# Project stage of a state-space and transformer kernel: matmuls to delta, B, C two tiles behind, statistics behind the taps, a wait in the load queue

## What is computed

```python
x = x + jnp.tanh(g_xattn[0]) * _L0_xattn_ref(ctx_1024, _layernorm(x, axis=-1), ...)
# inside, per batch b
x = jnp.einsum('ed,bld->bel', in_proj_w, hidden_states)      # 1024 channels from 512
xc = depthwise causal convolution of x, 4 taps
u = jax.nn.silu(xc + conv_b[None, :, None])
x_dbl = jnp.einsum('ke,bel->bkl', x_proj_w, u)               # 64 rows: delta's 32, B's 16, C's 16
delta = jax.nn.softplus(jnp.einsum('er,brl->bel', dt_proj_w, dt_lo) + dt_proj_b[None, :, None])
...                                                          # scan over l, then
y = y * jax.nn.silu(z)                                       # z is the layer norm of x
```

## Time and profile before

| what | us |
|---|---|
| median of 3 runs | 3019.37 (3013.48 to 3019.66) |
| time of the profiled execution | 3018.8 |
| its span | 3017.1 |
| project stage in it | about 172 |

### The profile page before, as it was taken

One profiled execution on the slowest core, in us unless ns is written; L12 is line 12 of the kernel. 1 busy time (PEld: TensorE's weight loads), 2 busy tenths in 40 slices (PEclk: granted clock), 3 DMA queues, 4 the chain that ended last, 5 costly groups with the idle time before them and its releaser, 6 DMA issues. The chain is left out here.

```text
span 3017.1 us, 30047 instructions
## 1 busy us (share of the span) xinstructions
PE 2392.6 (79%) x10552; PEld 1599.2 (53%) x10552; DVE 2110.9 (70%) x2626; ACT 1338.0 (44%) x2470; POOL 1683.2 (56%) x600
## 2 busy tenths in 40 slices
PE   7857777778777547986888888888883299999998
PEld 3334444444444326653767666654552186668863
DVE  4569999999999674432999999999997633310000
ACT  3457755566655342242665555665552212410000
POOL 1169999999999401003998898999993100000000
PEclk9969999989999758998999999999997599999999
DMA  7722252342522396745236335336333543144543
GB/s 259 253 90 75 67 158 77 113 139 63 164 66 60 115 374 208 287 134 189 84 105 197 99 104 186 109 98 216 98 108 133 204 170 98 50 144 151 152 153 104
DMA packets 224869, 426.70 MB, mean 141 GB/s; under 512 B 17488, under 2 KB 101712, under 8 KB 221904
## 3 DMA queue, kind: packets, MB, share of 16 engines
q1 hardware_dynamic: 211216, 368.68, 38.3%
q10 hardware_dynamic: 12160, 51.39, 4.3%
q0 software_dynamic: 1344, 4.72, 0.4%
HBM read 340.84 MB, written 83.89 MB: 141 GB/s over the span
## 5 line engine op out<-in xcount | busy, mean ns | idle before, releaser
L600 POOL TENSOR_TENSOR s_x<-s_du,k_bB 128x2048 f32<-128x2048 f32 x256 | 1156.3, 4533 | 80.8 <-PE s_py L663 52.0
L896 ACT ACTIVATE s_pA<-s_delta,k_negA 128x512 f32<-128x512 f32 x1024 | 664.1, 680 | 382.7 <-DVE s_x L947 373.9
L663 PE MATMUL s_py<-k_ident,s_x 128*128 128x128 f32 x4096 | 582.8, 289 | 260.6 <-DVE s_x L947 253.2
L663 PEld LDWEIGHTS s_py<-k_ident,s_x 128*128 128x128 f32 x4096 | 506.8, 150 | 489.3 <-DVE s_x L947 347.2
L962 DVE TENSOR_TENSOR_SCAN s_pA<-s_pA,s_x 128x512 f32<-128x512 f32 x384 | 452.2, 1214 | 40.9 <-POOL s_x L600 38.3
L947 DVE TENSOR_TENSOR s_x<-s_pA,k_bC 128x1024 f32<-128x1024 f32 x384 | 464.2, 1209 | 19.1 <-DMA k_bC<-scratch_xd 19.0
L962 DVE TENSOR_TENSOR_SCAN s_pA<-s_pA,s_carry,s_x 128x512 f32<-128x512 f32 x384 | 472.6, 1275 | 2.0 <-POOL s_x L600 1.6
L1570 PE MATMUL l_p<-l_hT,l_ring 128*128 128x256 f32 x1792 | 397.0, 381 | 2.5 <-DVE l_hT L1784 1.4
L1570 PEld LDWEIGHTS l_p<-l_hT,l_ring 128*128 128x128 f32 x1792 | 341.9, 191 | 50.2 <-issue 2.0
L607 POOL TENSOR_TENSOR s_x<-s_hp,k_bC 128x1024 f32<-128x1024 f32 x128 | 302.2, 2361 | 15.8 <-DVE s_hp L962 15.5
L1577 PE MATMUL l_p<-l_ring,l_hidden 128*128 128x512 f32 x512 | 220.9, 592 | 1.7 <-DMA l_ring<-in_wo 1.7
(11 more groups left out here) (200 smaller groups left out, 3100.1 us busy)
## 6 DMA issues: line engine op xcount, KB each, us to landing
k_bB<-scratch_xd SPq DMA_DIRECT2D x32, 1024.0 KB, 11.8
k_bC<-scratch_xd SPq DMA_DIRECT2D x32, 1024.0 KB, 12.3
scratch_ug<-p_ug ACTq DMA_DIRECT2D x16, 1024.0 KB, 4.0
k_u<-scratch_ug SPq DMA_DIRECT2D x64, 256.0 KB, 3.6
s_gy<-scratch_ug SPq DMA_DIRECT2D x64, 256.0 KB, 4.2
s_xt<-in_x SPq DMA_DIRECT2D x64, 256.0 KB, 4.6
scratch_x<-s_xt SPq DMA_DIRECT2D x64, 256.0 KB, 3.2
r_x<-scratch_x SPq DMA_DIRECT2D x32, 512.0 KB, 11.4
```

Source lines behind the costliest of these rows:

```text
L600: pool.tensor_tensor(out=x[:, 4 * g:4 * g + 4], in0=du[:, s % 2:s % 2 + 1].broadcast_to([P, 4, HALF]), in1=bB[:, 4 * g:4 * g + 4], op=ALU. ...
L663: last = nc.tensor.matmul(py[:, a], x[:, n, a * P:(a + 1) * P], ident[:], is_transpose=True, start=False, stop=is_last and a == HALF // P - 1)
L896: nc.scalar.activation(pA[:, n % 4], delta[:, s % 2], ACT.Exp, scale=negA[:, s % NE, n:n + 1]).then_inc(dA_ready, 1)
```

## The change

- `x_dbl(k - 2)` instead of `x_dbl(k - 1)` stands behind the projection of tile k, with a buffer more for u and the gate: `U_BUFS` is 3. `X_AHEAD` goes from 8 to 6.
- The three taps of a tile stand in a row, and all statistics of the next tile behind the third.
- SyncE waits for the second half of the first context before it loads more than `conv`. The x tile 0 now goes ahead of the rest of `w_in`. `w_x` has a semaphore of its own, for which TensorE alone waits, ahead of X(0).
- `copy_out(0)` stands behind tile 9's work instead of tile 8's.

```diff
-X_AHEAD = 8
+X_AHEAD, U_BUFS = 6, 3
...
-    ug = sb("ug", [P, 2, 2, L])
+    ug = sb("ug", [P, U_BUFS, 2, L])
...
+            sp.dma_start(conv[:], t["conv"]).then_inc(weights, 16)
+            sp.wait_ge(ctx_first[1], 16)
+            load_x(0)
             sp.dma_start(w_in[:, :, 2 * P:], t["w_in"][:, :, 2 * P:]).then_inc(w_in_rest, 16)
-            load_x(0)
+            sp.dma_start(w_x[:], t["w_x"]).then_inc(w_x_in, 16)
             load_x(1)
-            sp.dma_start(conv[:], t["conv"]).then_inc(weights, 16)
-            sp.dma_start(w_x[:], t["w_x"]).then_inc(weights, 16)
...
-                if k == 0:
-                    pe.wait_ge(weights, 32)
-                else:
-                    x_dbl(k - 1)
-            x_dbl(STEPS_NOW - 1)
+                if k == 2:
+                    pe.wait_ge(w_x_in, 16)
+                if k >= 2:
+                    x_dbl(k - 2)
+            for k in range(STEPS_NOW - 2, STEPS_NOW):
+                x_dbl(k)
...
-            act.wait_ge(weights, 32)
+            act.wait_ge(weights, 16)
...
-                at_least(act, ug_out[j], 16 * (k // 2))
-                at_least(act, xd_sums, k - 1)
+                at_least(act, ug_out[n], 16 * (k // U_BUFS))
+                at_least(act, xd_sums, k - U_BUFS + 1)
...
-                if k == NE:
+                if k == NE + 1:
                     copy_out(0)
...
-                    if i == 0 and k == 0:
-                        make_shift(0)
-                    if k + 1 < STEPS_NOW:
-                        (take_stats, take_mean, make_shift)[i](k + 1)
+                if k + 1 < STEPS_NOW:
+                    take_stats(k + 1)
+                    take_mean(k + 1)
+                    make_shift(k + 1)
```

More of the change, by code:

```diff
@@ L125, in project_stage @@
     ps_d = ctx.enter_context(nc.psum_tensor("p_xdp", [H2 * ND, HALF], F32))
-    w_in_ready, w_in_rest, weights, ctx_in = sem("w_in_r"), sem("w_in_rest"), sem("weights"), sem("ctx1")
+    w_in_ready, w_in_rest, weights, w_x_in, ctx_in = sem("w_in_r"), sem("w_in_rest"), sem("weights"), sem("w_x_in"), sem("ctx1")
     ctx_first = [sem(f"ctx0{h}") for h in range(H2)]
@@ L132, in project_stage @@
     u_ready, gate_ready, xd_sums, xd_copied, xd_out = sem("u"), sem("gate"), sem("xd_sums"), sem("xd_copied"), sem("xd_out")
-    ug_out = [sem(f"ug_out{j}") for j in range(2)]
+    ug_out = [sem(f"ug_out{j}") for j in range(U_BUFS)]
     exponent, small, made, kept, kept_chain = (sem(n) for n in ("exponent", "small", "made", "kept", "kept_chain"))
@@ L168, in _ @@
             sp.wait_ge(xd_out, 32 * SPAN)
-            for j in range(2):
-                sp.wait_ge(ug_out[j], 16 * STEPS_NOW // 2)
+            for j in range(U_BUFS):
+                sp.wait_ge(ug_out[j], 16 * len(range(j, STEPS_NOW, U_BUFS)))
         @block.gpsimd
@@ L193, in x_dbl @@
                 for h in range(H2):
-                    last = nc.tensor.matmul(ps_d[h * ND:(h + 1) * ND, :], w_x[:, e, :], halves(ug[:, k % 2, 0], h),
+                    last = nc.tensor.matmul(ps_d[h * ND:(h + 1) * ND, :], w_x[:, e, :], halves(ug[:, k % U_BUFS, 0], h),
                                             start=e == 0, stop=e == NE - 1)
@@ L229, in copy_out @@
                                   xd[h * ND:(h + 1) * ND]).then_inc(xd_out, 16)
-            act.wait_ge(weights, 32)
+            act.wait_ge(weights, 16)
             act.wait_ge(pads, 2)
             for k in range(STEPS_NOW):
-                e, j = k % NE, k % 2
+                e, j, n = k % NE, k % 2, k % U_BUFS
                 act.wait_ge(projected, k + 1)
@@ L283, in _ @@
                     take_mean(0)
-                    dve.wait_ge(weights, 32)
+                    make_shift(0)
+                    dve.wait_ge(weights, 16)
                     dve.wait_ge(pads, 2)
@@ L290, in _ @@
                         dve.wait_ge(taps, 3 * k + i)
-                    nc.vector.scalar_tensor_tensor(out=ug[:, j, 0], in0=raw[:, j, i:i + L], scalar=conv[:, e, i:i + 1],
-                                                   in1=ug[:, j, 0], op0=ALU.mult, op1=ALU.add).then_inc(taps, 1)
-                    if i == 0 and k == 0:
-                        make_shift(0)
-                    if k + 1 < STEPS_NOW:
-                        (take_stats, take_mean, make_shift)[i](k + 1)
+                    nc.vector.scalar_tensor_tensor(out=ug[:, n, 0], in0=raw[:, j, i:i + L], scalar=conv[:, e, i:i + 1],
+                                                   in1=ug[:, n, 0], op0=ALU.mult, op1=ALU.add).then_inc(taps, 1)
+                if k + 1 < STEPS_NOW:
+                    take_stats(k + 1)
+                    take_mean(k + 1)
+                    make_shift(k + 1)
 NPAIR = NS // 2
```

8 lines of the change are left out of this document (4 added, 4 removed).

## The result

| | before | changed |
|---|---|---|
| median of 5 runs, us | 3015.84 (3013.48 to 3019.66) | 2995.95 (2987.73 to 2998.47) |
| ratio, 95% interval | | 0.9924 (0.9904 to 0.9943) |
| profiled execution, us | 3018.8 | 2988.98 |
| its span | 3017.1 | 2987.3 |
| next stage starts at | 172.33 | 151.78 |

The kernel is faster by 19.9 us by the medians and by 22.9 us by the ratio. The forecast was 3000.1, a gain of 19.3. Two questions are open at this point: whether the steps inside the stage were right, and where the other 9.2 of the 29.8 us between the two profiled spans come from, since the next stage starts only 20.55 us earlier.

A forecast was written before the change was run, and what follows sets the result against it. The prediction took ScalarE and VectorE, passing one tile back and forth, to bound the project stage. Statistics 17.4, silu(0) 1.3 and an earlier start 0.6 sum to 19.3 us: from 3019.4 to 3000.1, range 2994 to 3007.

The forecast's parts named there:

- The ring of ScalarE and VectorE: Project stage: the two engines pass one tile back and forth and set the pace, 9.00 us a tile.
- The statistics: Moved behind VectorE's taps: 1.24 us less in each of 14 tiles, 17.4 us, plus 1.3 us at silu(0).
- cover: VectorE's 3.80 us wait before its first tap, said to hide the estimated 2.6 us of statistics at no cost.
- The lead of TensorE: Projections finish 2.8 us before ScalarE needs them, shrinking 0.29 us a tile, 0.5 left at tile 10, lasting to the end.
- The third buffer: One more buffer for u: ScalarE's first tap waits for a store three tiles old, not two; effect nothing.
- The head: Stage start, new load order: TensorE starts at 9.3 instead of 10.10; 0.6 us gained, from -0.6 to 2.3.
- off the path: At P(1): removing TensorE's 0.71 us wait for `w_x` was said not to affect the stage's time.
- the slow phase of P(0): TensorE's first five records or so, at half speed; starting 0.8 us earlier was to give 0.4 to 0.8 us.
- The sum: 17.4 + 1.3 + 0.6 = 19.3 us gained, giving 3000.1 from the median of 3019.4.
- the spread of the runs: Range term for whole executions: up to 6 us below the median.
- the rivals: TensorE as bound 0.16 (3005); late loads at the start 0.10 (3006.8); gain lost behind the stage 0.03 (3019); slow clock 0.03 (3116).

The follow-up runs named there:

- the head alone: Kernel before with only SyncE's wait, x tile 0 ahead of the rest of `w_in` and `w_x`'s own semaphore, run twice: 3023.03 and 3016.45 us.
- the third's: Changed kernel, unchanged, third profile and third set of times: ratio to the kernel before 0.992 (0.9907 to 0.9934), median 2990.95 us.

## Why the prediction was right, and where it failed

**What bounds.** Right. The ring of ScalarE and VectorE set the pace: the statistics alone brought 14.3 us, the matmuls two behind alone nothing.

**The statistics.** Right in size: 7.76 us a tile forecast and measured, silu(0) 1.3 us nearer to its first tap. Their cover is 1.37 us wide, where 3.80 - 2.6 gave 1.2, and the experiment with more statistics went through it.

**The lead of TensorE.** Right. The forecast took 8.05 us for TensorE's tile, and measured are 8.07; it had 0.5 us left at tile 10, and measured are 0.9, of which 0.3 come from the pause of ScalarE behind silu(7). That pause stood in no term of the forecast and cost 0.3 us. Behind the copy the lead lasted as said, down to 0.14 us at tile 15. TensorE's wait there was 1.62 us, not 1.3, and its clock did not fall.

**The third buffer.** "Nothing" was right for the changed kernel, but the reason given, that no store had held ScalarE before, says nothing of a faster ring. Statistics alone, with two buffers, lost 1.68 us to a store.

**The head.** 0.8 us earlier was taken for TensorE's start and 0.6 of it for the stage. Over all profiles the start is 0.5 us earlier, and silu(0), set right for the statistics, 0.3: 26.2 on average in the seven profiles with wait and late statistics, against 26.5 in the four with the old queue (three of them less 1.32). The first profile of the changed kernel had 2.1. The sentence that the removed wait for `w_x` is "off the path" was wrong for the head alone: it makes a gap behind which the clock falls, for 1.9 us, and in the changed kernel P(2) fills the gap. That 2.58 MB had moved when a load with 1.57 MB up to its end landed is what the trace shows; that the later loads took its time was not tested, and whether wait or order brings the half microsecond stays open. For the slow phase of P(0) the forecast had that a start 0.8 us earlier gives 0.4 to 0.8; measured, the phase lasts 3 to 6 us by itself, which moves silu(0) by more than the shift of the start does.

**The sum.** The stage gained 20.55 us in the first pair of profiles and 19.2 us by the means of two and three, against 19.3 forecast. That the mean comes so near is in part luck, since the start of the next stage moves by 0.9 us in the kernel before and by 1.6 in the changed one. The three ratios say 22.9, 17.8 and 24.1 us; the forecast's gain is inside their intervals but for the third's, 0.9907 to 0.9934, which begins at 19.9 us.

**What failed** is the step from the gain to a time, and with it the range. The sum's 19.3 us were taken from a level of 3019.4, the median of three runs ("That execution lies 0.6 below the median of 3019.4"). That level was high: the five runs of the first set have their median at 3015.84, and the later sets of the kernel before have 3015.33, 3015.53 and 3013.73, so it is 4 to 6 us lower. The same 19.3 us from 3015 give 2996, and the changed kernel's medians are 2995.95, 2997.52 and 2990.95. The first set's ratio puts it at 2992.9, below the range. The second part of the step is the term "the spread of the runs (up to 6 us below the median)". It was taken from three runs, while the part behind the stage alone moves by 12 us from execution to execution, and the 2.3 us that the head might bring were not added to it: 3000.1 - 6 is the 2994 of the range. By the lower level and both terms the lower end is near 2988 (2996 - 6 - 2.3), an estimate; single executions of the changed kernel went down to 2987.73.

None of the rivals came true in the changed kernel. TensorE did not set the pace in any tile, though at the last its lead was down to 0.14 us.

## What to carry to other kernels

When two engines hand a tile back and forth, look for work in their ring that somebody else doesn't wait for, and put it into the idle time behind the hand-over; the price of doing so can be read from the last tile, where that work is missing. Moving a third engine off the ring is worth nothing while it has slack, and is what keeps the gain once the ring is shorter, so add up its own tile before cutting. When a single tile is slow, read in the row who ended the wait before giving the time to the engine that looks closest to the bound. Before turning a gain into a time, ask how far executions of the same kernel lie apart in the parts that are not touched, and make the range at least so wide.

## What the runs showed of the hardware

In the project stage, all gaps of 3.27 us and more between TensorE's matmuls were followed by a granted clock of 0.50, and one of 1.62 us by 1.00. After gaps of 2.00 and 2.01 us at the same place of the same kernel the clock fell once and stayed once, and nine of the ten gaps from 2.00 to 2.80 us kept it. In the version with the last tile in halves two records behind a gap of 2.58 us had 1.00, and the two behind the next gap, of only 1.16 us, had 0.50.

TensorE's first weight loads of the program stood 0.86 us apart, the later ones 0.43, with a granted clock of 1.00 shown for both. The phase lasted 3 us in one profile of the kernel before and 6 us in both of the head alone.

ScalarE issued the store behind silu(7) 1.46 us after that silu in nine profiles of kernels with three buffers for u, and 1.14 us after it in five with two. No other tile shows this.

GpSimd's root of 128 x 1 took 1.53 us beside a tap of VectorE and 0.55 us with VectorE idle.

The same program's part behind the stage took 2834.3 to 2846.6 us in 14 executions. Between the first two traces it arose in steps of 3 us at single units, one of them beside a wait of GpSimd of 8.83 us for a load of B, where the other trace has 6.13 us of idle time; what makes the difference was not tried.
